# Last sixteen steps of a two-layer triangle kernel: turned pairs and their copies alternate between two places, and the mixing product is done as 64-row, 64-column products into two banks

## The reference, cut to what matters

```python
left = jax.nn.sigmoid(x @ left1) * (x @ left2)
right = jax.nn.sigmoid(x @ right1) * (x @ right2)
p = jnp.einsum('nsre,nkre->nske', left, right)
p = _layernorm(p, ln2_w, ln2_b)
g = jax.nn.sigmoid(jnp.einsum('nsrz,zy->nsry', x, gate))
q = jnp.einsum('nrse,ez->nsrz', p, out_w) * g
return residual + q
```

## Time and profile before

| what | value |
|---|---|
| median of three runs | 949.6 us |
| the profiled execution's own time | 949.63 us |
| its span, first to last instruction | 947.8 us |
| TensorE busy, weight loads busy | 85%, 82% |
| VectorE, ScalarE, GpSimd busy | 77%, 67%, 56% |
| first mix of the last sixteen steps starts | 900.55 us |
| last mix starts | 941.97 us |

### The profile page before, as it was taken

How to read it: one execution, slowest core, us unless ns; L and a number is a source line. 1 busy time by engine, 2 the same in 40 slices (tenths; PEclk the granted TensorE clock), 3 DMA queues, 4 the chain that set the end, 5 groups by cost and what they waited for, 6 DMA issues and landing times.

```text
span 947.8 us, 25568 instructions
## 1 busy us (share of the span) xinstructions
PE 808.2 (85%) x9308; PEld 774.8 (82%) x9308; DVE 729.9 (77%) x2122; ACT 632.4 (67%) x881; POOL 531.8 (56%) x428
## 2 busy tenths in 40 slices
PE   3765555677999899989999999899999999999776
PEld 2654445677999899979999998899999899989775
DVE  6789979787599949992788998619970998078796
ACT  4899979766677547743567676547754776267675
POOL 3548979767266407640764444316760667068776
PEclk9689989999999999999999999999999999999999
DMA  4235665468999539868666779848981895977686
GB/s 123 57 91 151 183 193 168 154 211 314 373 294 335 154 101 289 287 203 328 233 209 202 222 245 332 302 134 251 309 255 47 232 309 184 305 250 234 207 274 200
DMA packets 154451, 211.92 MB, mean 224 GB/s; under 512 B 10712, under 2 KB 92888, under 8 KB 152280
## 3 DMA queue, kind: packets, MB, share of 16 engines
q1 hardware_dynamic: 153464, 210.18, 69.5%
q10 hardware_dynamic: 864, 0.12, 0.1%
HBM read 126.37 MB, written 83.89 MB: 222 GB/s over the span
## 4 chain that ended last, share of the span: by engine, by line
PE 43%; DVE 22%; DMA 12%; issue 10%; ACT 8%; POOL 3%; SPq 1%; DVEq 0%; POOLq 0%; ACTq 0%
PE bank L1364 18%; PE ps_w L1404 7%; DVE stats L1096 7%; DMA xin<-in_x_dram 6%; PE bank L1344 4%; PE bank L1345 4%; PE ps_t L1386 4%; DVE xc L1184 2%; PE ps_x L1415 2%; DMA xin<-x 2%; DMA xt<-xt 2%; DVE rhs L1063 1%; DVE split L1191 1%; DVE ps_t L1184 1%; DVE lhs L1063 1%
## 5 line engine op out<-in xcount | busy, mean ns | idle before, releaser
L778 POOL TENSOR_TENSOR rstd<-var,minus_half 128x8 f32<-128x8 f32 x112 | 192.9, 1722 | 260.9 <-DVE var L1157 260.9
L1364 PE MATMUL bank<-rhs,lhs 128*128 128x128 f32 x1536 | 224.9, 279 | 12.0 <-issue 5.8
L1364 PEld LDWEIGHTS bank<-rhs,lhs 128*128 128x128 f32 x1536 | 197.7, 194 | 13.9 <-issue 8.1
L795 POOL TENSOR_TENSOR xc<-xin,stats 128x504 f32<-128x504 f32 x128 | 139.0, 1086 | 58.4 <-DVE split L1191 53.1
L1415 PE MATMUL ps_x<-ident_b,split 128*128 128x128 bf16 x1024 | 84.1, 229 | 64.2 <-DVE split L1191 41.0
L879 ACT ACTIVATE sig<-bank 128x512 f32<-128x512 f32 x192 | 115.0, 609 | 32.8 <-PE bank L1345 31.7
L1415 PEld LDWEIGHTS ps_x<-ident_b,split 128*128 128x128 bf16 x1024 | 68.1, 103 | 74.4 <-DVE split L1191 46.3
L1096 DVE BATCH_NORM_STATS2 stats<-xin 128x6 f32<-128x128 f32 x512 | 118.8, 283 | 10.5 <-DMA xin<-in_x_dram 10.3
L917 ACT ACTIVATE xt<-ps_x 128x1024 bf16<-128x1024 bf16 x96 | 98.1, 1022 | 41.3 <-PE ps_x L1415 39.3
L1404 PE MATMUL ps_w<-w_out,opair 128*128 128x128 f32 x832 | 114.1, 280 | 11.5 <-ACT opair L901 10.5
L1404 PEld LDWEIGHTS ps_w<-w_out,opair 128*128 128x128 f32 x832 | 105.1, 193 | 15.7 <-ACT opair L901 14.1
(11 more groups left out here) (154 smaller groups left out, 2167.3 us busy)
## 6 DMA issues: line engine op xcount, KB each, us to landing
chunk<-xt SPq DMA_DIRECT2D x80, 512.0 KB, 4.8
xin<-in_x_dram SPq DMA_DIRECT2D x128, 256.0 KB, 3.4
xt<-xt SPq DMA_DIRECT2D x64, 512.0 KB, 5.3
x<-xin SPq DMA_DIRECT2D x64, 256.0 KB, 4.7
xin<-x SPq DMA_DIRECT2D x64, 256.0 KB, 4.9
out_dram<-xin SPq DMA_DIRECT2D x64, 256.0 KB, 4.6
spill<-lhs SPq DMA_DIRECT2D x8, 1024.0 KB, 7.7
chunk<-xcol SPq DMA_DIRECT2D x16, 512.0 KB, 4.9
```

Source lines behind the costliest of these rows:

```text
L778: g.tensor_tensor(rstd[:, m % 2], var[:, m % 2], minus_half[:, :], ALU.pow).then_inc(rooted, 1)
L795: g.tensor_tensor(xc[:, h, :, lo:], src[:, :, lo:], stats[:, m % 4, :, 1:2].broadcast_to([P, COLS, C - lo]), ALU.subtract).then_inc(centre ...
L1364: last = mm(bank[:, n], operand_of(q // 4, "lhs", kh)[:, c, :], operand["rhs"][:, kh, c, :], start=kh == 0, stop=kh == HALVES - 1)
```

## The change

Three things are done for steps 176 to 191, and nothing elsewhere.

1. For odd steps the turned pairs go to `ps_w` in place of `ps_t` and the copy of them to `opair_3` (the unused `staged` tile) in place of `opair`. The waits are loosened to the step before the last: `turn` waits for `turn_out(m-2)`, `turn_out` for `mix(m-2)`.
2. The mixing products go to `banks[1]`, the first 256 words of each of its two banks, and `scale` reads them there.
3. A mixing product is that of one token: 64 rows (half of a pair's partitions) by out_w's own 64x64 block, 64 columns. There are eight of them in place of four. Those of partitions 0 to 63 write the one bank, those of 64 to 127 the other, in turn.

```diff
         def opair_of(m):
+            if m >= LAST_BASE and m % 2:
+                return opair_3
             return opair_2 if PAIRED <= m < P_BASE and m % 2 else opair[:, :, :]
         def pairs_of_buffers(m):
-            return 2 if PAIRED <= m < P_BASE else 1
+            return 2 if PAIRED <= m < P_BASE or m > LAST_BASE else 1
+
+        opair_3 = staged[:, 0].bitcast(F32).rearrange("p (n k) -> p n k", k=P)
+        ps_w_pairs = ps_w[:, :, :].rearrange("p (n a) c -> p n (a c)", a=2)
+
+        def turned_in(m):
+            return ps_w_pairs if m >= LAST_BASE and m % 2 else ps_t[:, :, :]
+
+        def mixed_in(m):
+            if m < LAST_BASE:
+                return ps_w[:, :, :].rearrange("p (n a) c -> p n a c", a=2)
+            return banks[1][:, :, 0:P * 2].rearrange("p a (n c) -> p n a c", c=C)
...
             def turn(m):
                 o, c0 = m - X_BASE, step(m)[3]
-                pe.wait_ge(turned_out, after(o - 1))
+                pe.wait_ge(turned_out, after(o - 2 if m > LAST_BASE else o - 1))
+                if m == LAST_BASE + 1:
+                    pe.wait_ge(scaled, after(m - 2 - P_BASE))
...
             def mix(m):
+                if m == LAST_BASE:
+                    pe.wait_ge(quad_done, after(8 * GROUPS_C - 1))
+                for n in range(COLS // 2 if m >= LAST_BASE else 0):
+                    for b in range(2):
+                        rows = slice(C * b, C * (b + 1))
+                        last = mm(mixed_in(m)[:, n, b], opair_of(m)[rows, n, :], w[rows, rows],
+                                  start=True, stop=True)
+                for n in range(COLS // 2 if m < LAST_BASE else 0):
                     last = mm(ps_w[:, 2 * n:2 * n + 2, :], opair_of(m)[:, n, :], w[:, :],
```

More of the change, by code:

```diff
@@ L900, in turn_out @@
                 else:
-                    a.activation(opair_of(m), ps_t[:, :, :], ACT.Identity, scale=ln2[:, 0:1],
+                    a.activation(opair_of(m), turned_in(m), ACT.Identity, scale=ln2[:, 0:1],
                                  bias=ln2[:, 1:2]).then_inc(turned_out, 1)
@@ L1197, in scale @@
                 dve.wait_ge(mixed, after(m - X_BASE))
-                v.tensor_tensor(gt[:, h], ps_w[:, :, :], gt[:, h], ALU.mult).then_inc(scaled, 1)
+                v.tensor_tensor(gt[:, h].rearrange("p (n a) c -> p n a c", a=2), mixed_in(m),
+                                gt[:, h].rearrange("p (n a) c -> p n a c", a=2), ALU.mult).then_inc(scaled, 1)
             for t in range(T_END):
@@ L1385, in turn @@
                 for n in range(COLS // 2):
-                    last = nc.tensor.transpose(ps_t[:, n, :], src[:, n], ident[:, :])
+                    last = nc.tensor.transpose(turned_in(m)[:, n, :], src[:, n], ident[:, :])
                 last.then_inc(turned, 1)
@@ L1402, in mix @@
                     pe.wait_ge(scaled, after(m - P_BASE - 1))
-                for n in range(COLS // 2):
+                if m == LAST_BASE:
[6 more added lines that the diff above has]
+                for n in range(COLS // 2 if m < LAST_BASE else 0):
                     last = mm(ps_w[:, 2 * n:2 * n + 2, :], opair_of(m)[:, n, :], w[:, :],
```

## The result

The changed kernel takes 965.2 us (median of four runs, 964.5 to 966.5); the kernel before, run beside it, 949.3 us. The ratio is 1.0182, with a 95% interval of 1.0148 to 1.0217: the change makes the kernel 1.8% slower, some 16 to 17 us. The prediction said 950.8 us with a range of 947.2 to 963.

A forecast was written before the change was run, and what follows sets the result against it. It took a two-step loop of waits to bound the kernel: TensorE with ScalarE, then ScalarE alone. Places 0, mixing products 0 and row mode 8 x 0.15 = +1.2 us on 949.63 gave 950.8 us, range 947.2 to 963.

The forecast's parts named there:

- What bounds the kernel: Steps 176 to 191: a loop of waits repeating every two steps, 5.42 us a pair, no engine full.
- A to B: From ScalarE's copy of an even step to the next odd step's: 2.46 us, set by TensorE and ScalarE.
- B to A: From an odd step's copy to the next even step's: 2.96 us, ScalarE alone, TensorE having 0.40 us of slack.
- The alternating places: Loosened waits of turn and turn_out in steps 176 to 191: implied by waits that remain, gain 0.
- The mixing products, loads side by side: Mix of steps 176 to 191: loads of the two row halves overlap, so it stays at 0.88 us, change 0.
- Up to 2x: Skill's speedup for contracted dimension 64 or less: mix would take 0.44 us; the prediction held the load rows against it.
- 16 x 0.11: The mix's 16 weight loads one after another at 2.4 GHz: 1.77 us, 0.88 more than before.
- The change of row mode: Turn's first load waits for the last 64-row mixing product: 0.15 us later, paid eight times, +1.2 us.
- Rival 1, loads in a row: Mix's weight loads follow one another, mix 1.77 us, TensorE becomes the bound: +12.8, 962.4 us; chance 0.30 with partial overlaps.

The follow-up runs named there:

- The run with the gap filled: The whole change plus 44 unread bf16 products once in TensorE's idle stretch ahead of step 176: 947.5 us, ratio 0.9984 to the kernel before.
- the run of 128 columns: The changed kernel, still 64-row products with halves in turn, but each moves 128 columns, zero block included (one moves 64): 952.3 us, ratio 1.0018.

## Why the prediction was wrong

**What bounds the kernel.** Right: the loop of copy, mix and turn from A to B, ScalarE from B to A. The run with the gap filled shows both distances, 2.57 and 2.95 us.

**The alternating places: 0.** Right, 0.9992 of before. The reason was right as well, since moving the turn did change the time. What I gave for such a move, a gain of at most 2.4 us, left out a loss: it cost 8 us, because I looked only at TensorE's and ScalarE's order and not at VectorE's scaling ahead of the root.

**The mixing products, loads side by side: 0.** The mechanism was right: 16 loads in 0.97 us at 2.4 GHz, and the runs with the halves one after the other and with full rows show that it is the overlap. The rule of the Trainium skill, "TensorE: Matmul & The Clock Gate", Part 3, The mechanism, that different row groups overlap, agrees with these runs. For the "Up to 2x" of the Trainium skill's "TensorEngine Tiling (Array Packing)", Theoretical Speedup, the prediction had set the wrong pair against each other. Sixteen loads take 1.86 us one after the other (full rows, 2.4 GHz) and 0.97 in turns, so the factor shows between these two. It brings nothing against the kernel before, whose eight loads of 128 rows serve two tokens at once and fill the same 0.97 us.

**Where it failed.** The step is "16 x 0.11" with what stands ahead of it, "a granted clock of 1.00, that is 2.4 GHz". I priced every term at that level because the windows of the kernel before show it from 906.85 us on. The first row of the same group shows 0.62 for 898.5 to 903: right behind TensorE's idle stretch the clock falls to 1.2 GHz, and in the kernel before it comes back while the turn of 177 runs, behind the mix of step 176. That return was an effect of the work I was about to replace, and I took it as given. No term and no rival of the prediction had the clock in it. What the runs show in its place is 16 loads in 1.79 us at a granted clock of 0.50, and 3.89 us a step in place of 2.71 on the average of the pair. From the mix of step 176 to that of 191 it is 58.3 us (898.52 to 956.82) in place of 41.4 (900.55 to 941.97), 16.9 more, and 0.9 more from there to the end; 0.3 less goes to the first turn, which still ran at 1.00. That is the 17.5 of the stretch.

**The change of row mode: +1.2.** Right in kind. The turn's first load comes 1.04 us after the mix's first in place of 0.88, and A to B is 2.57 in place of 2.46: 0.11 a time, 0.9 us in all, in place of 0.15 and 1.2. B to A hides it, as said. That the turn waits for the last mixing product fits with the run of 128 columns, where the load comes 0.05 us later still, the difference that the prediction put between the two widths, and with the run of the places alone, which writes one of the same banks with 128 rows and has 0.89.

**Rival 1, loads in a row, 962.4 us**, came nearest to the measured time and is wrong. Its copies, 3.5 us apart, would have been at 2.4 GHz with loads in a row; measured are 3.89 us at 1.2 GHz with loads side by side. Its price of such loads was good: 1.77 us forecast, 1.86 in the run with full rows after the clock's return. Had I had only the median, the nearness of the two numbers would have made it the explanation. The load spacing against the granted clock tells them apart in two rows.

**The range** ended at 963 and so below the result; the chance of slower, 0.47, rested on the wrong mechanism. Where the forecast failed is a condition under all its terms, not the size of one.

## What to carry to other kernels

Before rows at one clock level are used to price a change, look where in the stretch the clock rises, and ask whether the work that was running when it rose is still there after the change. Products that cost hardly anything more at 2.4 GHz (0.4 to 0.9 us here) can still take twice as long, when they follow an idle stretch and the clock doesn't come back under them. Putting harmless full products into that stretch is a cheap test of whether a loss is the clock's.

## What the runs showed of the hardware that I had not expected

- TensorE stayed at 0.50 for more than 60 us while the profile had it busy for 32.43 of 32.55 us. With fp32 products of 64 rows and 64 columns, and the turns and gate products between them, the clock held at 1.00 when it was there (run with the gap filled) and didn't return when it wasn't.
- fp32 loads follow each other at about 0.21 us at 1.2 GHz and 0.11 at 2.4, with 64 rows and with 128. Loads for the two halves of the rows run two at a time in turns (1.79 us for 16 at 1.2 GHz), and even when the halves stand one after the other in the program, some loads of the second start early (2.69 us for 16, not 3.4).
- Products of 64 columns over all 128 rows took 3.49 us for 16 loads at 1.2 GHz and 1.86 at 2.4, and there the clock came back after some 55 us, which I can't explain.
